# A decoder layer on one core: the four small PSUM banks shared in whole turns, the shared FFN's gate and up on score pair 1, the running expert counts added by VectorE, and a new order on every engine

## What is computed

```python
x = x + attn(layernorm(x))                 # rotary positions, causal, Wq Wk Wv Wo
x = x + xattn(layernorm(x), ctx)           # 77 context rows per batch
x = x + ffn(layernorm(x))

# ffn: 7 routed experts of 512 hidden columns, and one shared expert for all tokens
probs = softmax(x @ router_w)              # 8 columns
top1_val, top1_idx = top_k(probs, 2)[..., 0]
hid    = (x @ up_w[e]) * silu(x @ gate_w[e])
routed = hid @ down_w[e]  where e == top1_idx        # column 8 has no expert
shared = ((x @ shared_up_w) * silu(x @ shared_gate_w)) @ shared_down_w
return 2.0 * top1_val * routed + shared
```

## Time and profile before

| | |
|---|---|
| time, median of 3 runs | 1065.71 us (1065.3 to 1066.14) |
| span of the profiled execution | 1065.7 us |
| PE busy | 992.5 us, 93% of the span |
| DVE busy | 870.9 us, 82% |
| ACT busy | 737.2 us, 69% |
| POOL busy | 631.4 us, 59% |
| chain that ended last | PE 76%, DVE 10%, issue 4%, SPq 3% |

### The profile page before, as it was taken

One profiled execution on the slowest core, in us unless ns is written; L12 is line 12 of the kernel. 1 busy time (PEld: TensorE's weight loads), 2 busy tenths in 40 slices (PEclk: granted clock), 3 DMA queues, 4 the chain that ended last, 5 costly groups with the idle time before them and its releaser, 6 DMA issues.

```text
span 1065.7 us, 45022 instructions
## 1 busy us (share of the span) xinstructions
PE 992.5 (93%) x16200; PEld 818.3 (77%) x16201; DVE 870.9 (82%) x2853; ACT 737.2 (69%) x1557; POOL 631.4 (59%) x1488
## 2 busy tenths in 40 slices
PE   1579999999999999999999999999999999999995
PEld 1357777777777777777777777777777889999995
DVE  4367999999999999999999999999986457777774
ACT  0267878888888878888888888887875145555552
POOL 0346677777777677777777777767764124444443
PEclk9999999999999999999999999999999899999998
DMA  6222011000100010000100010000000122222220
GB/s 133 71 72 77 28 32 32 26 30 26 32 26 30 25 29 28 26 30 26 32 26 30 26 29 28 30 25 28 28 29 21 58 70 70 73 71 68 70 65 5
DMA packets 66648, 44.27 MB, mean 42 GB/s; under 512 B 24135, under 2 KB 61451, under 8 KB 66592
## 3 DMA queue, kind: packets, MB, share of 16 engines
q1 hardware_dynamic: 55424, 30.35, 10.5%
q0 software_dynamic: 5312, 12.18, 3.3%
q10 hardware_dynamic: 5856, 0.99, 0.7%
HBM read 23.96 MB, written 18.29 MB: 40 GB/s over the span
## 4 chain that ended last, share of the span: by engine, by line
PE 76%; DVE 10%; issue 4%; SPq 3%; DMA 2%; ACT 1%; POOL 1%; ACTq 1%; DVEq 0%; POOLq 0%
PE pv L1122 11%; PE scores L1302 6%; PE scores L1307 6%; PE ro L1318 6%; PE ro L1177 6%; PE scores L1163 5%; PE st L1232 5%; DVE arena L641 4%; PE scores L999 4%; PE scores L1169 4%; PE ro L1139 3%; PE pj L1145 3%; PE ro L1131 3%; PE ro L1150 2%; PE scores L1033 2%
## 5 line engine op out<-in xcount | busy, mean ns | idle before, releaser
L919 ACT ACTIVATE arena<-scores 128x1024 f32<-128x1024 f32 (+1 forms) x256 | 262.6, 1026 | 48.5 <-PE scores L1016 33.6
L641 DVE TENSOR_REDUCE arena<-scores 128x8 f16<-128x1024 f32 (+1 forms) x256 | 256.7, 1003 | 47.5 <-PE scores L1007 37.6
L859 ACT ACTIVATE arena<-st 128x128 f16<-128x128 f16 (+2 forms) x256 | 154.9, 605 | 7.9 <-PE st L1232 6.8
L859 ACT ACTIVATE arena<-arena 128x512 f16<-128x512 f32 (+2 forms) x192 | 92.9, 484 | 70.3 <-POOL arena L453 50.3
L1122 PE MATMUL pv<-arena 128*32 128x128 f32 (+1 forms) x4096 | 139.3, 277 | 0.0
L1122 PEld LDWEIGHTS pv<-arena 128*32 128x32 f32 (+1 forms) x4096 | 104.6, 110 | 17.1 <-issue 10.1
L439 POOL TENSOR_TENSOR arena<-arena,neg_half 128x1 f32<-128x1 f32 x192 | 106.5, 555 | 15.0
L449 POOL TENSOR_TENSOR arena<-arena 128x256 f32<-128x256 f32 x64 | 46.4, 725 | 78.9 <-DVE arena L633 78.9
L526 POOL DMA_INDIRECT out_dram<-x_tile x70 | 69.9, 998 | 38.5 <-POOL carried L525 26.1
L477 POOL TENSOR_TENSOR arena<-arena 128x128 f32<-128x128 f32 x128 | 51.7, 404 | 61.2 <-DVE arena L651 61.2
L1232 PE MATMUL st<-id,arena 128*128 128x128 f16 (+1 forms) x1024 | 74.0, 215 | 8.5 <-POOL arena L462 8.5
(11 more groups left out here) (175 smaller groups left out, 2681.3 us busy)
## 6 DMA issues: line engine op xcount, KB each, us to landing
x_tile<-xs SPq DMA_DIRECT2D x70, 129.0 KB, 2.0
arena<-arena SPq DMA_DIRECT2D x512, 4.0 KB
arena<-in_x_dram SPq DMA_DIRECT2D x64, 64.0 KB, 1.8
out_dram<-pay SPq DMA_DIRECT2D x64, 64.0 KB, 1.6
arena<-in_ctx_dram SPq DMA_DIRECT2D x64, 38.5 KB
w_gate<-in_L_ffn_gate_w_dram SPq DMA_DIRECT2D x7, 256.0 KB, 2.8
w_up<-in_L_ffn_up_w_dram SPq DMA_DIRECT2D x7, 256.0 KB, 3.1
w_down<-in_L_ffn_down_w_dram SPq DMA_DIRECT2D x7, 256.0 KB, 4.0
```

What stands on the lines that cost most here:

```text
L641: v.tensor_reduce(nmax[:, n, :].rearrange("p (m r s) -> p r m s", r=2, s=SLOT)[:, u, :, 0:HG], pair(s)[:, :, 0:HG * keys].rearrange("p m ( ...
L859: return a.activation(to, of, ACT.Copy)
L919: a.activation(e32[0:rows, 2 * n + u, :], scores[0:rows, 1024 * s:1024 * (s + 1)], ACT.Exp).then_inc(sexp_done[n][u], 1)
```

## The change

No product of the attention or the FFN changes. What changes is who uses which bank, how the router's marks and counts are formed, and the order of nearly every line.

**Banks.** The four single banks are used in whole turns: each piece starts at column 0 of its bank and waits until the readers of the piece ahead of it in that bank are done. `pv` has the first transposes, `project_qkv`, `positions` and `shared_down`; `pj` the second transposes, the context's transposes, the router, the cross-attention's maxima, values and the self-attention's `stacks`; `st` `project_kv2`, `stacks2` and the cross-attention's output projection; `ro` the third transposes, `project_q2`, the self-attention's output projection, maxima and values. On the score pairs, all u = 1 fills are on pair 0, all u = 0 fills and gate and up on pair 1.

**Counts and marks.** `positions` is left with its two fp16 products; DVE adds the running count. The marks are formed with tensor operands spread over the eight columns, in three instructions in place of two. Two of four `carry` copies a batch go.

```diff
-LAG = 11
-LATE = 56
+LATE = 60
...
 def positions(b, p):
-    cols = ro[:, 2 * P:2 * P + 2 * E].rearrange("p (n e) -> p n e", n=2)
-    t.matmul(cols, id32[:, :], run_base[:, :].unsqueeze(1).to_broadcast([P, 2, E]), start=True, stop=False,
-             skip_group_check=True)
-    t.matmul(cols[:, 0], earlier[:, :], hot16[:, p, :], start=False, stop=False, skip_group_check=True)
+    cols = pv[:, 0:2 * E].rearrange("p (n e) -> p n e", n=2)
+    t.matmul(cols[:, 0], earlier[:, :], hot16[:, p, :], start=True, stop=False, skip_group_check=True)
     last = t.matmul(cols[:, 1], ones16[:, :], hot16[:, p, :], start=False, stop=True, skip_group_check=True)
...
 def run_of(b, p):
     wait(dve, pos_psum, b + 1)
-    v.tensor_copy(run_base[:, :], ro[:, 2 * P + E:2 * P + 2 * E]).then_inc(run_ready, 1)
+    v.tensor_tensor(run_pos[:, p, :].rearrange("p (n e) -> p n e", n=2), run_pos[:, 1 - p, E:2 * E].unsqueeze(1).to_broadcast([P, 2, E]),
+                    pv[:, 0:2 * E].rearrange("p (n e) -> p n e", n=2), ALU.add).then_inc(run_ready, 1)
...
+def same_of(b, p):
+    wait(dve, top_ready, b + 1)
+    v.tensor_tensor(same[:, :], logits[:, p, :], top[:, p:p + 1].to_broadcast([P, E]), ALU.is_equal).then_inc(same_ready, 1)
+
 def marks_of(b, p):
-    wait(dve, top_ready, b + 1)
-    v.scalar_tensor_tensor(out=mark[:, :], in0=logits[:, p, :], scalar=top[:, p:p + 1], in1=marks,
-                           op0=ALU.is_equal, op1=ALU.mult).then_inc(marked, 1)
+    wait(dve, same_ready, b + 1)
+    v.tensor_tensor(mark[:, :], same[:, :], marks, ALU.mult).then_inc(marked, 1)
...
 def hot_of(b, p):
     wait(dve, mark_topped, b + 1)
-    v.tensor_scalar(hot16[:, p, :], mark[:, :], mark_top[:, :], None, ALU.is_equal).then_inc(hot_ready, 1)
+    v.tensor_tensor(hot16[:, p, :], mark[:, :], mark_top[:, :].to_broadcast([P, E]), ALU.is_equal).then_inc(hot_ready, 1)
...
+pos_turns = (((rot_ready, 8), (val_ready, 8),), ((xT_ready[0], 8),), ((sh_added, 0),), ((run_ready, 0),),)
+pr1_turns = (((qkT2_ready, 3),), ((k2_ready, 3), (val2_ready, 3),), ((resid_done[1], 0),),)
...
 def step(i, p):
-    at(i, p, 5, project_kv2, ((xT_ready[0], 4),), ((ctxT_ready, 1),), ((val_ready, 3),), ((val2_ready, 0),))
+    at(i, p, 4, project_kv2)
```

More of the change, by code:

```diff
@@ L291, in pair, with run @@
             return scores[:, 1024 * s:1024 * (s + 1)].rearrange("p (m c) -> p m c", m=2)
-        def run(eng, step):
-            first = (LAG + 3) // 2
+        def run(eng, step, lag):
+            first = (lag + 3) // 2
             for i in range(2 * first):
@@ L301, in run @@
                 step(2 * pair + 1, 1)
-            for i in range(NB, NB + LAG):
+            for i in range(NB, NB + lag):
                 step(i, i % 2)
@@ L1110, in two_turns, with stack4 @@
                         round2(s2, u2, p2, g)
-            def values(b, p, n, *users):
-                vals, rows = ((val, P), (val2, C))[n]
-                wait(pe, sexp_done[n][0], b + 1)
-                wait(pe, sexp_done[n][1], b + 1)
-                turn(pe, b, *users)
+            def stack4(bank, to, src, rows, step):
+                for g in range(HG):
+                    last = t.transpose(bank[:, to + g * step:to + g * step + rows], src[0:rows, g * P:(g + 1) * P],
+                                       id16[0:rows, 0:rows])
+                return last
@@ L1176, in shared_down @@
+            def shared_down(b, p):
+                turn(pe, b, *down_turns)
                 for c in range(FC):
-                    last = t.matmul(ro[:, P:2 * P], hidT[:, 0, c * P:(c + 1) * P], ws_down[:, c, :], start=c == 0, stop=c == FC - 1)
+                    last = t.matmul(pv[:, 0:D], hidT[:, 0, c * P:(c + 1) * P], ws_down[:, c, :], start=c == 0, stop=c == FC - 1)
                 last.then_inc(sh_psum, 1)
-            def early(i, lag, piece, *args):
-                if isinstance(i, int) and 4 <= i < lag:
-                    piece(i - lag, *args)
@@ L1187, in busy_scores, with early, late, busy_gate @@
+            def early(i, lag, piece):
+                if isinstance(i, int) and 2 <= i < lag:
+                    piece(i - lag)
+            def late(i, lag, piece):
+                if isinstance(i, int) and NB <= i - lag and i <= NB + 8:
+                    piece(i - lag)
+            def busy_gate(b):
+                turn(pe, b, *gate_turns)
                 for c in range(FC):
-                    t.matmul(scores[:, 1024 * s + c * P:1024 * s + (c + 1) * P], w_qkv[:, 0:P], w_qkv[:, 0:P], start=True, stop=True)
@@ L1190, in busy_rows, with busy_down @@
-            def busy_rows(b, *users):
-                turn(pe, b, *users)
+                    t.matmul(pair1[:, c * P:(c + 1) * P], w_qkv[:, 0:P], w_qkv[:, 0:P], start=True, stop=True)
+            def busy_down(b):
+                turn(pe, b, *down_turns)
                 for c in range(FC):
-                    t.matmul(ro[:, P:2 * P], w_qkv[:, 0:P], w_qkv[:, 0:P], start=c == 0, stop=c == FC - 1)
-            def late(i, lag, piece, *args):
-                if isinstance(i, int) and NB <= i - lag and i <= NB + 11:
-                    piece(i - lag, *args)
@@ L1200, in busy_pj, with over @@
-            def busy_pj(b, *users):
+                    t.matmul(pv[:, 0:D], w_qkv[:, 0:P], w_qkv[:, 0:P], start=c == 0, stop=c == FC - 1)
+            def over(b, users):
                 if all(b + user[0][1] > NB for user in users):
@@ L1220, in ctxT_of @@
-            def ctxT_of(b, p, *users):
-                turn(pe, b, *users)
-                wait(pe, ctx_in_s[p], 8 * b + 16 - 8 * p)
-                t.transpose(pj[:, 3 * D:3 * D + C], ctx_t[0:C, p, :], id32[0:C, 0:C]).then_inc(ctxT_psum, 1)
-            def project_kv2(b, p, *users):
-                turn(pe, b, *users)
-                wait(pe, ctxT_ready, b + 1)
-                t.matmul(pj[0:C, 0:2 * D], ctxT[:, 0:C], wc_kv[:, :], start=True, stop=True).then_inc(kv2_psum, 1)
-            def stack4(to, src, rows, step):
-                for g in range(HG):
-                    last = t.transpose(st16[:, to + g * step:to + g * step + rows], src[0:rows, g * P:(g + 1) * P],
-                                       id16[0:rows, 0:rows])
-                return last
```

687 lines of the change are left out of this document (396 added, 291 removed).

## The result

The changed kernel takes 1085.01 us (median of 4 runs, 1083.14 to 1089.75) against 1065.93 us before; the ratio is 1.0198 (95% interval 1.0176 to 1.0221). It is slower by 2%, where 1037 us was forecast.

What follows compares the result with a forecast made beforehand. PE was taken to bound the first stage at 11.95 us a step; -0.56 us a step over 57 full steps is -32, plus 3 for fill and drain: 1065.7 - 32 + 3 = 1037 us, range 1020 to 1062.

Steps and rivals of the forecast that it cites:

- The step that failed: Other engines: DVE, ACT, SP and POOL don't hold PE while under 11.4 us a step; DVE falls to about 10.4.
- PE bounds the first stage: First stage: PE, busy 491.5 of 500 us, sets the step of 11.95 us; only its own row can gain.
- The marks: Router on DVE: three new operations at 0.15 us each, 0.45 for 0.875, priced by L712's 144 ns.
- The marks are dear: Rival: each mark operation costs L691's 0.497 us, DVE has 11.4 us of work a step; 1060 us, chance 0.07.
- points 2 and 4: PE's waits of the second transposes for x1 (0.29 us) and self-attention's output projection for shared_down's readers (0.09) go.
- point 3: Cross-attention's output projection on PE: its late start behind up's last matmul goes, 0.20 us a step.
- three new neighbours: PE's new changes between full array and tiles, 0.10 us each: +0.30, less 0.10 for one that goes.
- The new wait for `values_in`: On PE, positions in bank pv waits for values_in to be read: 0.13 to 0.22 us a step, taken as 0.15.
- PE's sum: PE per step: -0.91 us lost, +0.20 for switches, +0.15 for a new wait, net -0.56.
- term 1: The fp32 product of the counts (L1214) leaves PE: 0.25 us a step less.
- Fill and drain: Pipeline's ends: fill to the first shared_down +6 us, drain -3 to -4, together +3 (ends -3 and +10).
- The slower one: Rival: cross-attention's row maxima return late through SP's DMAs, with 0.2 us to spare; 1075 us, chance 0.10 for over 1068.

Runs made afterwards that it cites:

- Two edits that open the ring: Changed kernel with add_cross_bias right behind ln2_rstd on POOL: 1062.15 us; changed kernel with the marks in their old two-operation form: 1060.83 us.
- three edits on POOL and DVE: Changed kernel with add_cross_bias early on POOL, marks in the old two operations, ln3_mean_var right behind its statistics on DVE: 1044.60 us.
- four more edits: Changed kernel with add_cross_bias early, plus marks in two operations, ln3_mean_var early, scatter behind self_scaled, positions behind the next stacks: 1024.28 us.

## Why the prediction was wrong, step by step

**The step that failed** is the sentence that DVE, ACT, SP and POOL are off PE's path as long as they keep under 11.4 us a step. They did keep under it: DVE's busy time is 452.55 / 41 = 11.0 us a step of 12.17 (not the 10.4 forecast: the marks took 0.6 more), POOL's 8.5. But a ring is closed by who waits for whom, and its length is the sum of work and hand-overs along it, whatever share of each engine it fills. The change wrote a new order for all engines, and the prediction checked it for PE's queue and for SP's trip alone. That add_attention waits for POOL's `add_cross_bias`, two lines from the end of POOL's step and behind the scatter, was in the code and was not followed. This bond is of the change's own making. In the kernel before the same addition stood third in POOL's step, ahead of ln3 and the scatter, and `add_attention` had no wait for it; the change moved the one and added the other (`wait(dve, xb_ready[1], b - 1)`), which the section on the change doesn't list. Two edits that open the ring gave 23 and 24 us, each alone; with more of it opened the time is 1044.60, 1032.21 and, with `positions` moved too, 1024.28.

The sentence that PE bounds the first stage failed with it: in the kernel before, 0.25 us less work on PE brought nothing (1067.69 us).

**The marks.** Forecast 0.45 us for three, measured 0.31 + 0.60 + 0.15 = 1.06 (means over the whole run), more than the 0.87 they replaced. The row taken as nearest, L712, reads PSUM, and the two rows that were taken as dear forms were in good part waits for POOL. All four are on one engine with nearly one shape; what tells them apart is where their inputs are and what POOL does just then. "The marks are dear" was a rival that came near the price (0.35 an operation on average, where it began to decide) by a wrong way: not DVE's sum of work, which stayed at 11.0, but one place of the ring. In the loop the marks ahead of `hidden_of` take 0.97 us (0.32 + 0.65) where the two old ones took 0.92; against the kernel before it is the ring that is new, not the wait.

**PE's side.** The waits for x1 and the shared sum are gone (points 2 and 4), and so is that of the cross-attention's output projection (point 3): the last matmul of up starts at 506.17, L1251 0.11 later. The starts in the timeline of after:

```profile
506.28 0.39 PE L1251 MATMUL st<-wc_o,arena 128*128 128x128 f32 x2
506.50 0.27 PE L1186 MATMUL pj<-id,arena 128*128 128x128 f32 x1
506.70 1.08 PE L1241 MATMUL ro<-arena 128*32 128x128 f32 x32
508.46 0.25 PE L1115 MATMUL scores<-arena 28*77 28x128 f16 x2 [0.67 <-DVE hidT L784]
```

A projection holds PE 0.22 where it held it 0.33, which was not forecast. From full-array transposes to values it is 0.20 (506.50 to 506.70) against 0.16, so 0.04 where 0.10 was taken; the kernel before had that row too, 0.21 from L1139 to cross rounds (509.03 to 509.24). Only one of the three new neighbours was read. The Trainium skill ("TensorEngine Tiling (Array Packing)", Key Properties) states that changing the tiling mode drains TensorE; these 0.04 us are all that the pair shows of it. The new wait for `values_in` was taken as 0.15: in the changed kernel the ring hides it, and when the ring was open, taking it away gave 0.17 a step. PE is busy 10.9 us a step where it was 11.7. So PE's sum was right in its signs and too small if anything; but PE's row is now 1.3 us a step shorter than its time, and term 1 by itself brought nothing in the kernel before.

**Fill and drain.** The first `shared_down` was taken as 6 us later and is 4.0 later. The ten steps behind it added 4.0 more; at 0.24 a step 2.4 would be the longer step, the rest was not priced.

**The rivals.** The slower one, row maxima too late, did not come: no wait of PE for a DMA stands among the waits of after. The outcome was on the slower side by a mechanism that was not among the rivals.

With the ring opened by three edits on POOL and DVE and the scatter one line later, the step is 11.33 and the time 1032 us, close to the forecast of 11.4 and 1037. That agreement is luck in part, since that version has the marks in their old form, and the product put back cost 5 us there and not 16.

## What to carry to other kernels

Before a change of order is priced, follow each wait of every engine around until it comes back to the same engine one step later, and add up the turn; a busy share below the step excludes nothing. A time in a row is a price only if nothing else was running that it could wait for: compare the ends of short DVE operations with the ends of POOL's. When PE idles behind another engine, look first for a line on the third engine that can move into its idle time; here one such line gave 2% of the changed kernel's time, and with four more edits it went 4% below the kernel before.

## What the runs showed of the hardware that was not expected

DVE operations with both inputs in SBUF wait for a large POOL operation (128x128 or 128x256) that has started, and end 0.02 to 0.03 us after it: 0.65 us for L748, where L756, of the same shape, took 0.15. The wait is counted in the operation's own time, not as idle time. L756 took its 0.15 beside one of POOL's 128x1 operations, which had started after it. DVE's transposes and statistics beside the same POOL operations (L710, 0.30 us; L636, 0.28) did not wait visibly.

POOL's indirect DMA starts 0.50 us after the small operation ahead of it in the changed kernel, as the timeline and the waits (L512, 20.5 us over 41) have it, and 0.17 in the loop of the kernel before (7.1 over 42); with the ring opened it is 0.33 on average (14.6 over 44). What decides it was not tried.

Two-matmul projections of 128x128 hold PE 0.22 us in the changed kernel and 0.33 before, at one granted clock of 1.00. What decides that was not tried either.
